# Cross attention: keys and values made and quantised early in the program, queries handled two tiles at a time, expert weights loaded in two places

## The reference, cut to what matters

```python
q = (x @ Wq + bq).reshape(1, B * N, H, hd)             # 16 heads of 16
kv = (cond @ Wkv + bkv).reshape(1, -1, 2, H, hd)
k, v = (kv[:, :, 0], kv[:, :, 1])
q = jnp.transpose(q * scale, (0, 2, 1, 3))
q = _fq_sym(q, axis=-1)                                 # round(x / s) clipped to +-127, s = max|x| / 127 of a head's row
k = _fq_sym(k, axis=-1)
v = _fq_sym(v, axis=2)                                  # s over all 1024 rows
attn = jnp.einsum('bhqd,bhkd->bhqk', q, k)
attn = _fq_unsigned(jax.nn.softmax(attn), axis=-1)
out = jnp.einsum('bhqk,bhkd->bhqd', attn, v)
out = jnp.transpose(out, (0, 2, 1, 3)).reshape(B, N, C)
return out @ Wp + bp
```

## Time and profile before

| | us |
|---|---|
| median of 3 runs | 1160.37 (1157.77 to 1161.32) |
| the profiled execution: its time | 1160.59 |
| its span | 1159.0 |
| PE busy | 840.3 |
| DVE busy | 782.7 |
| ACT busy | 490.5 |
| POOL busy | 547.7 |

### The profile page before, as it was taken

One profiled execution on the slowest core, in us unless ns is written; L12 is line 12 of the kernel. 1 busy time (PEld: TensorE's weight loads), 2 busy tenths in 40 slices (PEclk: granted clock), 3 DMA queues, 4 the chain that ended last, 5 costly groups with the idle time before them and its releaser, 6 DMA issues. The chain is left out here.

```text
span 1159.0 us, 13028 instructions
## 1 busy us (share of the span) xinstructions
PE 840.3 (72%) x4490; PEld 556.9 (48%) x4513; DVE 782.7 (68%) x1296; ACT 490.5 (42%) x703; POOL 547.7 (47%) x394
## 2 busy tenths in 40 slices
PE   5678989767678678677778477956667676569990
PEld 2343744356566566566632464532333343447760
DVE  4764220499999999999624684849999997424442
ACT  2212022454654654554411231368888886112220
POOL 2116000689879879879210223017777775150005
PEclk9768989878788788788879787986876776579995
DMA  3010030000000000000020004906999887033114
GB/s 127 1 73 0 1 115 1 1 1 1 1 1 0 1 1 1 1 1 1 1 96 0 1 1 173 292 17 128 178 186 171 175 165 163 2 110 127 55 59 123
DMA packets 155442, 73.84 MB, mean 64 GB/s; under 512 B 138813, under 2 KB 151297, under 8 KB 154178
## 3 DMA queue, kind: packets, MB, share of 16 engines
q1 hardware_dynamic: 153842, 68.81, 24.2%
q0 software_dynamic: 1536, 4.20, 1.2%
HBM read 27.90 MB, written 11.53 MB: 34 GB/s over the span
## 5 line engine op out<-in xcount | busy, mean ns | idle before, releaser
L680 POOL TENSOR_TENSOR r_pairs<-r_side_exp 128x1035 f32<-128x1035 f32 x128 | 248.3, 1972 | 9.5 <-DVE r_w L845 8.4
L735 PE MATMUL r_head_sum<-ident,r_w 128*128 128x128 f32 (+1 forms) x1024 | 154.3, 316 | 86.4 <-ACT r_w L763 63.0
L763 ACT ACTIVATE r_w<-r_w,r_scale 128x1001 f32<-128x1001 f32 (+1 forms) x128 | 144.4, 1139 | 163.4 <-DVE r_w L845 141.7
L735 PEld LDWEIGHTS r_head_sum<-ident,r_w 128*128 128x128 f32 (+1 forms) x1024 | 141.1, 168 | 107.3 <-ACT r_w L763 81.2
L1529 ACT ACTIVATE c_probs<-c_scores,c_bias,c_q_scale 128x1024 int16<-128x1024 f32 x128 | 154.2, 1205 | 34.9 <-DVE c_bias L1542 26.2
L1540 DVE TENSOR_REDUCE c_neg_max<-c_scores 128x1 f32<-128x1024 f32 x128 | 155.5, 1215 | 13.6 <-PE c_scores L1480 13.4
L1467 POOL CAST c_rounded<-c_probs 128x1024 bf16<-128x1024 int16 x128 | 132.2, 1041 | 47.8 <-ACT c_probs L1529 45.7
L837 DVE SCALAR_TENSOR_TENSOR r_chosen<-r_pairs,r_kept,r_z 128x1024 f32<-128x1024 f32 (+1 forms) x112 | 141.3, 1275 | 12.5 <-ACT r_sims L747 4.3
L1480 PE MATMUL c_scores<-c_kT,c_placed 128*128 128x512 bf16 x233 | 98.2, 507 | 62.7 <-ACT c_probs L1529 54.8
L845 DVE TENSOR_TENSOR r_w<-r_pairs,r_chosen 128x1024 f32<-128x1024 f32 (+1 forms) x112 | 134.8, 1204 | 0.0
L711 PE MATMUL r_head_sum<-r_up,r_wT 128*128 128x256 f32 (+1 forms) x256 | 74.7, 463 | 13.4 <-ACT r_wT L774 13.4
(11 more groups left out here) (271 smaller groups left out, 1415.4 us busy)
## 6 DMA issues: line engine op xcount, KB each, us to landing
ew_w<-in_w SPq DMA_DIRECT2D x2, 2992.0 KB, 13.2
sorted_rows<-ew_w SPq DMA_DIRECT2D x1, 4096.0 KB, 39.1
e_row<-sorted_rows SPq DMA_DIRECT2D x8, 512.0 KB, 8.1
expert_rows<-e_made SPq DMA_DIRECT2D x8, 512.0 KB, 2.9
ew_w<-in_w_near SPq DMA_DIRECT2D x1, 2176.0 KB, 22.2
ctxT<-in_ctxT SPq DMA_DIRECT2D x2, 1024.0 KB, 8.6
r_up<-in_up SPq DMA_DIRECT2D x1, 2048.0 KB, 9.7
c_pT<-c_rounded SPq DMA_TRANSPOSE x128, 2.8
```

Of the source, the lines that this page charges most:

```text
L680: nc.gpsimd.tensor_tensor(pairs[:, v % MADE, :].rearrange("p (a b) -> p a b", b=KEYS), a.broadcast_to([P, ROWS, KEYS]), b.broadcast_to([P, ...
L735: last = nc.tensor.matmul(head_sum[0:m, b // 4, (b % 4) * P:(b % 4 + 1) * P], w[:, v % RING, b * P:b * P + m], ident[:, :], start=(h == 0 ...
L763: nc.scalar.activation(w[:, v % RING, 0:COLS[f]], w[:, v % RING, 0:COLS[f]], ACT.Silu, scale=scale[:, t % 2, h:h + 1]).then_inc(silu_done, 1)
```

## The change

Keys and values of the cross attention are projected in `linear_attention`: 12 items (8 tiles of k, 4 blocks of v) on PE, nine of them between the two halves of the sums and three behind the output projection, taken by ACT. `load_context` moves there, with no second load of ctxT, and k's bias is loaded to all 128 rows and added by DVE. Their quantisation (`quantise_context`) goes to `private_state`, before the wait for `sims_ready`. `identb` and the zeroing of the fourth part move to the program's start, the zeroing of `placed` and the placing of tile 0 into `quantise`. In `quantise` PE turns k and v between its steps for x, q is projected without the bias matmul, and DVE takes q from PSUM with its bias and quantises it in four pairs of tiles. The first half of `w13` and the zeros move to `convolve`, from a zeroed buffer of their own, and its block ends only when the zeros have landed; `w2_far` is a tensor of 48 rows. `rounded` in `attend` reuses the parts' memory, `o` and `oT` that of xT.

```diff
@@ linear_attention @@
             sp.dma_start(w_out[:, :, :], i["w_out"]).then_inc(loaded, 16)
+            load_context(sp, sh, i)
             load_tokens(sp, sh, i)
...
         def _(pool):
+            nc.gpsimd.memset(sh.kv.parts[:, :, :, PARTS - 1, :], 0.0).then_inc(sh.kv.zeroed, 1)
             norm_pool(nc, pool, ln, 0)
...
+            def context(n):
+                if n >= 2:
+                    pe.wait_ge(cw.taken, n - 1)
+                g, j = divmod(n, 3)
+                for d in range(DC):
+                    if j < 2:
+                        t = 2 * g + j
+                        last = nc.tensor.matmul(ln.turned[:, n % 2, 0:D], sh.ctxT[:, d, t * P:(t + 1) * P], cw.w_kv[:, d, 0:D],
+                                                start=(d == 0), stop=(d == DC - 1))
+                    else:
+                        c, h = divmod(g, NH)
+                        last = nc.tensor.matmul(ln.turned[:, n % 2, :], cw.w_kv[:, d, D + c * P:D + (c + 1) * P],
+                                                sh.ctxT[:, d, h * HALF:(h + 1) * HALF], start=(d == 0), stop=(d == DC - 1))
+                last.then_inc(cw.made, 1)
...
@@ private_state @@
             norm_vector(nc, dve, ln, x, chain)
+            quantise_context(nc, dve, chain, sh.cw, sh.kv)
             dve.wait_ge(sims_ready, 1)
@@ convolve @@
-            load_context(sp, sh, i)
             for dst, src in ((s.w_o[:, :, :], "w_o"), (s.b_o[:, :], "b_o"), (s.proj[:, :], "proj")):
                 sp.dma_start(dst, i[src]).then_inc(s.loaded, 16)
+            sp.wait_ge(zeros_ready, 1)
+            load_expert_near(sp, sh.ew, i, zeros[:, :, :])
+            sp.wait_ge(sh.ew.zeroed, 16)
@@ quantise @@
+            turn(0)
+            turn(1)
+            for t in range(NT):
+                turn_x(t)
+                turn(t + 2)
+                if t == 1:
                     pe.wait_ge(loaded, 16 * len(loads))
+                if t >= 1:
+                    project(t - 1)
+            project(NT - 1)
+            for t in range(NT):
+                pe.wait_ge(q_whole, t // QT + 1)
+                turn(KV + t)
...
+            for g in range(NT // QT):
+                at = slice(g * QT, (g + 1) * QT)
+                for t in range(g * QT, (g + 1) * QT):
+                    dve.wait_ge(rows_ready, t + 1)
+                    nc.vector.scalar_tensor_tensor(q[:, t, :], row[:, t % 2, 0:D], HD_C ** -0.5, b_q[:, :],
+                                                   ALU.mult, ALU.add).then_inc(rows_taken, 1)
+                dve.wait_ge(rows_taken, (g + 1) * QT)
+                head_scales(nc, chain, q, at, s.q_scale, q_inverse)
+                chain.step(nc.vector.tensor_tensor(head_rows(q, at), head_rows(q, at), by_head(q_inverse, at), ALU.mult))
+                chain.step(nc.vector.tensor_scalar(q[:, at, :], q[:, at, :], ROUND, ROUND, ALU.add, ALU.subtract))
+                dve.wait_ge(turned_ready, at.stop)
+                whole = kv.parts[:, at, :, :, :].rearrange("p t h r d -> p (t h) r d")
+                chain.step(nc.vector.tensor_scalar(whole[:, :, 0, :], head_rows(q, at), LEVELS, -LEVELS, ALU.min, ALU.max))
+                nc.vector.tensor_copy(whole[:, :, 1:PARTS - 1, :],
+                                      whole[:, :, 0:1, :].broadcast_to([P, QT * HEADS_C, PARTS - 2, HD_C])).then_inc(q_whole, 1)
@@ mix_experts @@
-                    last = nc.tensor.matmul(y[:, u % 2, 0:D], gatedT[:, u % 2, c, :], right, start=(c == 0), stop=(c == 1))
+                    last = nc.tensor.matmul(y[:, u % 2, 0:D], gatedT[0:(P, FAR)[c], u % 2, c, :], right, start=(c == 0), stop=(c == 1))
```

More of the change, by code:

```diff
@@ L258, in _ @@
             pe.wait_ge(inverse_ready, 1)
+            pe.wait_ge(cw.taken, CONTEXT_FIRST)
             for t in range(NT):
@@ L277, in _ @@
                 last.then_inc(out_ready, 1)
+            for n in range(CONTEXT_FIRST, CONTEXT_ITEMS):
+                context(n)
         @block.scalar
@@ L293, in _, with take_context @@
                 n += 1
+            def take_context(n):
+                act.wait_ge(cw.made, n + 1)
+                g, j = divmod(n, 3)
+                if j < 2:
+                    nc.scalar.copy(cw.k[:, 2 * g + j, :], ln.turned[:, n % 2, 0:D]).then_inc(cw.taken, 1)
+                else:
+                    c, h = divmod(g, NH)
+                    nc.scalar.activation(cw.vT[:, c, h * HALF:(h + 1) * HALF], ln.turned[:, n % 2, :], ACT.Identity,
+                                         bias=cw.b_v[:, c:c + 1]).then_inc(cw.taken, 1)
+            act.wait_ge(cw.loaded, CONTEXT_LOADS)
+            for n in range(CONTEXT_FIRST):
+                take_context(n)
             for h in range(NH):
@@ L1241, in _ @@
-            nc.gpsimd.memset(s.ones[:, :], 1.0).then_inc(zeroed, 1)
-            nc.gpsimd.memset(sh.ew.w2[:, 1, :, :], 0.0).then_inc(sh.ew.padded, 1)
+            nc.gpsimd.memset(s.ones[:, :], 1.0).then_inc(ones_ready, 1)
+            pool.wait_ge(ln.normed, ln.tiles + NT)
+            for half in range(2):
+                for own in range(2):
+                    at = slice(own * P // 2, (own + 1) * P // 2)
+                    nc.gpsimd.memset(s.placed[at, half, :, 1 - own, :], 0.0).then_inc(s.placed_zeroed, 1)
@@ new lines, in turn_x, with project @@
+            def turn_x(t):
+                pe.wait_ge(ln.normed, ln.tiles + t + 1)
+                if t >= 2:
+                    pe.wait_ge(ln.copied, ln.tiles + t - 1)
+                for c in range(DC):
+                    last = nc.tensor.transpose(ln.turned[:, t % 2, c * P:(c + 1) * P], ln.xn[:, t, c * P:(c + 1) * P], ident[:, :])
+                last.then_inc(ln.turned_ready, 1)
+            def project(t):
+                pe.wait_ge(ln.copied, ln.tiles + t + 1)
+                if t >= 2:
+                    pe.wait_ge(rows_taken, t - 1)
+                for c in range(DC):
+                    last = nc.tensor.matmul(row[:, t % 2, 0:D], xT[:, c, t * P:(t + 1) * P], w_q[:, c, :],
+                                            start=(c == 0), stop=(c == DC - 1))
+                last.then_inc(rows_ready, 1)
@@ L1320, in _, with copy_x @@
+            def copy_x(t):
+                act.wait_ge(ln.turned_ready, ln.tiles + t + 1)
+                nc.scalar.copy(xT[:, :, t * P:(t + 1) * P], ln.turned[:, t % 2, 0:D].rearrange("p (c n) -> p c n", c=DC)).then_inc(ln.copied, 1)
+            copy(0)
+            for t in range(NT):
+                copy_x(t)
+                copy(t + 1)
+            for n in range(NT + 1, KV + NT):
+                copy(n)
         @block.vector
@@ L1361, in _ @@
-            dve.wait_ge(cols_taken, DC * NH)
-            chain.step(nc.vector.tensor_reduce(s.v_scale[:, :], vT[:, :, :], AX.X, ALU.max, apply_absolute_value=True))
-            chain.step(nc.vector.tensor_scalar(s.v_scale[:, :], s.v_scale[:, :], 1.0 / LEVELS, SCALE_LEAST, ALU.mult, ALU.max))
-            chain.step(nc.vector.reciprocal(v_inverse[:, :], s.v_scale[:, :]))
-            for c in range(DC):
-                last = nc.vector.tensor_scalar(vT[:, c, :], vT[:, c, :], v_inverse[:, c:c + 1], ROUND, ALU.mult, ALU.add)
@@ L1367, in _ @@
[L1367 to L1379 removed]
+            dve.wait_ge(loaded, 16 * len(loads))
@@ L1382, in attend, with place_queries @@
+def place_queries(nc, s, t):
+    for own in range(2):
+        at = slice(own * P // 2, (own + 1) * P // 2)
+        nc.gpsimd.tensor_copy(s.placed[at, t % 2, :, own, :], s.qT[at, :, t * P:(t + 1) * P]).then_inc(s.q_placed, 1)
 def attend(nc, sh, s):
```

308 lines of the change are left out of this document (139 added, 169 removed).

## The result

| | before | after |
|---|---|---|
| median of 4 runs, us | 1159.53 | 1130.49 |
| lowest to highest, us | 1157.77 to 1161.32 | 1120.38 to 1135.93 |
| profiled execution, us (its span) | 1160.59 (1159.0) | 1125.34 (1123.6) |

The ratio is 0.9738, with a 95% interval of 0.9686 to 0.9790: faster by 29 us where 39 to 40 were forecast. The median lies 1.5 us above the range's upper end, the profiled execution inside it. Two of the four runs, 1135.6 and 1135.9, lie 10 to 16 us above the others, so half of this median is theirs; the kernel before has no such run in the 54 of this case. In six later runs the same kernel had a median of 1125.84 and one run at 1136.07.

A forecast was written before the change was run, and what follows sets the result against it. Stages stand one behind the other, so each saves what its own longest path loses. -38.6 - 0.6 - 0.9 = -40.1 on the profiled 1160.59 gives 1120.5, median 1120.3 us; range 1117 to 1124, chance 0.42.

The forecast's parts named there:

- rival 5: Experts: the 48-row half of down keeps the clock at 0.50, some 82 us of work double, 1202 us; chance 0.02.
- Quantise: Quantise stage: without the key and value work, first score at 744.6 instead of 783.17, -38.6 us.
- rival 3: Quantise: full clock early, by tile 1, so the first pair is taken 3.0 us earlier, 1117.3 us; chance 0.13.
- the row of 10.3 us of work at 0.50: Quantise before: PE busy 10.30 of the first 11 us at clock 0.50, taken as evidence against an early rise.
- Rival 2: Quantise: half clock throughout, PE sets the pace, -33.6 us and 1125.3 us; chance 0.15.
- the placing: Quantise: POOL's placing of tile 0 beside pair 2 or 3 holds DVE for 0 to 2.1 us, taken 1.0.
- Private state: Private state: quantising keys and values, 29.4 us, fits DVE's wait of 31.27 with 1.9 to spare, 0 us.
- Rival 6: Private state: the DVE work is not hidden, if over 36.5 us; a quarter more gives 1120.6 us; chance 0.02.
- Linear attention: Linear attention: nine projections in PE's wait, three behind; sums start 0.8 later but run at full clock, -0.6 us.
- Rival 1: Linear attention: full clock throughout, so the stage ends 4.9 us earlier, 1115.4 us; chance 0.17.
- Token experts: Start of the next stage: PE just busy, so ACT waits less for it, 0 to -1.6 us, taken -0.9.
- Transfers: Convolve: zeros and 3 MB of weights issued at about 589 land by 628, before 637.37, 0 us.

The follow-up runs named there:

- before48: The kernel before with only the second half of down reading 48 rows instead of 128: 1170.78 us, ratio 1.0105.
- the second profile: A second profile of the changed kernel, run again with no edit; median of its six runs 1125.84 us.
- zeros3: The changed kernel with the zeros written three times in convolve, one after the other: 1129.84 us, ratio 0.9758.
- after_deep: The changed kernel with only the head projections of convolve made 128 rows deep, down still 48: 1125.95 us, ratio 0.9723.
- context0: The changed kernel with all twelve key and value projections behind linear attention's output, none before the second sums: 1140.74 us, ratio 0.9876.
- far128: The changed kernel with the second half of w2 padded with zeros and down 128 rows deep in both halves: 1115.32 us, ratio 0.9622.

## Why the prediction was wrong, point by point

- **The step that failed: `down`.** The prediction counted the experts at nothing and wrote that the units would be 2.5 us apart as before. It saw the 48 rows only as a risk for the clock (rival 5, 82 us or nothing). The clock stayed at 1.00, and the price was another: two exposed weight loads, 0.34 us a unit, 10.9 over the 32 sorted units and 11.8 in all (how the rest lies in the eight shared units is not read). The same edit alone on the kernel before (before48) costs 11.6. Nothing in the rows of the kernel before prices a switch of depth in a busy stretch, but the page of the Trainium skill named above would have made it a rival; the prediction weighed only what the depth does to the clock.
- **The number, and luck in it.** With that term the sum would have been 1132 for the median, above the range. The profiled execution lies at 1125.34 because 7 us of gains stand against the term that the sum did not have (quantise 2.5, block attention 3.5, token experts 1.3, private state 1.1, less 1.3 lost elsewhere). The median of the first four runs, 1130.49, is out of the range by the two high runs; the median of all ten runs of this kernel, 1125.84, is inside it. That would have been luck, with the experts wrong by 11.8.
- **Quantise: -41.1 for -38.6, the start of the pairs by luck.** The first pair began 11.1 us into the stage, as forecast, but by another way: the clock was at 1.00 3.7 us into the stage, which is rival 3, PE then stood for its weights, and the clock fell and rose once more. In the second profile and in those of zeros3, after_deep and context0, where this stage is the same, the first pair began 8.1 to 8.5 us in and the stage took 27.7 to 28.3 us. So rival 3, 3.0 us earlier, is what usually occurs, and the row of 10.3 us of work at 0.50 did not carry over. Rival 2 did not occur. Pairs of 4.1 for 4.7 made 1.8 of the rest, the placing, 0.5 for 1.0, another 0.5.
- **Private state: right**, 29.0 us for 29.4, 1.8 to spare for 1.9. Rival 6 counts the 1.9 twice: the wait of 31.27 and the gap of 3.3 give 34.6 and not 36.5, and a quarter more than 29.4 would have cost 2.2 us.
- **Linear attention: +0.4 for -0.6.** The sums gained 1.73 as forecast; the 0.5 of the inverses did not come, and L302 took 0.46 longer. Rival 1 did not occur: L295 took 7.19.
- **Token experts: -2.2 for -0.9.** PE's transposes ran at full clock and the clock rose again 2 us earlier in the first products (0.98 in 94 to 96 us, for 0.50 before). That this is the change's doing is not shown: before48, with the old linear attention, has 73.3 us here too.
- **Transfers: the sum right, the reason short.** The term says what the new place costs, 0. It does not say that the old place would have cost about 10 us in the changed kernel.
- **Block attention: not forecast in either direction.** -3.5 in one profile, 0 in the next, +12 in the profile of a high run of far128, all with the clock moving at another time. The range had no term for that, and the median of four runs fell out of it by 1.5.

## What to carry to other kernels

Count for every matmul whose rows change what stands before and behind it: one of 48 or 64 rows between ones of 128 cost 0.34 us here, 11.6 us over 40 units, and padding it with zeros to 96 or 128 rows brought that back, less 1 to 3 us in the stage where the zeroing stood. A transfer's price belongs to what runs beside it; when a stage shrinks, look again at what used to end inside it. And where PE has waits, give the clock's rise and fall a term in the range of its own: in quantise a wait of 1.82 us instead of 0.59 stood ahead of a fall, and the stage was 2.6 us longer.
